# Spreading a column of attention scores over the partitions by two DMAs instead of eight transposes

## The reference, cut to what matters

```python
Wh = einsum('bnf,fo->bno', h, W);  s1 = Wh @ a1;  s2 = Wh @ a2
e = s1[:, :, None] + s2[:, None, :]
e = where(e >= 0, e, 0.2 * e)
e = where(adj == 0, -inf, e);  attention = softmax(e, axis=-1)
h_prime = einsum('bij,bjo->bio', attention, Wh)
```

## Time and profile before

| | us |
|---|---|
| median of 3 runs (638.06 to 638.8) | 638.43 |
| span of the profiled execution, first to last instruction | 636.4 |
| PE busy | 621.6 (98%) |
| DVE busy | 474.8 (75%) |
| ACT busy | 433.8 (68%) |
| POOL busy | 167.4 (26%) |

### The profile page before, as it was taken

The page is one execution under the profiler, slowest core; times in us unless marked ns, Lnnn a source line. Parts: engine busy times, 40 slices in busy tenths (PEclk is TensorE's granted clock), DMA queues, the critical chain, the costliest instruction groups (busy, mean ns, idle before and its releaser), DMA issues.

```text
span 636.4 us, 9580 instructions
## 1 busy us (share of the span) xinstructions
PE 621.6 (98%) x2768; PEld 440.9 (69%) x2768; DVE 474.8 (75%) x1623; ACT 433.8 (68%) x995; POOL 167.4 (26%) x228
## 2 busy tenths in 40 slices
PE   9999999999999999999999999999999999999994
PEld 6756656447975687578658757865885687577794
DVE  4999999876847767866887787688768767465656
ACT  3667767966947766795677577557847766546774
POOL 1464551005233002304503240341143032103211
PEclk9999999999999999999999999999999999999998
DMA  8424000000000000000000000000000000000000
GB/s 337 142 115 166 1 1 1 1 0 2 2 1 1 0 2 0 2 2 33 2 0 2 34 1 2 33 2 1 1 33 2 2 28 6 1 1 33 2 35 33
DMA packets 4372, 16.84 MB, mean 26 GB/s; under 512 B 480, under 2 KB 480, under 8 KB 4192
## 3 DMA queue, kind: packets, MB, share of 16 engines
q1 hardware_dynamic: 4320, 16.23, 6.6%
HBM read 12.03 MB, written 4.19 MB: 26 GB/s over the span
## 4 chain that ended last, share of the span: by engine, by line
PE 76%; DVE 3%; ACT 2%; issue 1%; POOL 0%; POOLq 0%; ACTq 0%; DVEq 0%
PE QQ L831 26%; PE QQ L843 15%; PE PA L814 4%; PE PA L786 4%; PE PB L805 2%; PE PB L796 2%; PE PB L667 2%; PE PA L667 2%; PE PA L767 2%; PE PB L767 2%; PE QQ L865 1%; PE PB L884 1%; PE PB L746 1%; PE PA L746 1%; PE QQ L875 1%
## 5 line engine op out<-in xcount | busy, mean ns | idle before, releaser
L1200 ACT ACTIVATE raw<-QQ,BL 128x256 f32<-128x256 f32 (+2 forms) x279 | 150.1, 558 | 75.1 <-PE QQ L843 37.7
L831 PE MATMUL QQ<-HT,WT 128*128 128x256 f32 (+2 forms) x558 | 183.9, 474 | 1.1 <-ACT raw L1200 0.6
L446 POOL TENSOR_TENSOR RSD<-VAR,pw 128x4 f32<-128x4 f32 (+1 forms) x43 | 61.8, 1438 | 381.7 <-DVE VAR L1422 381.7
L831 PEld LDWEIGHTS QQ<-HT,WT 128*128 128x128 f32 x558 | 103.5, 190 | 59.2 <-issue 28.3
L843 PE MATMUL QQ<-HB,WT 128*128 128x256 f32 (+2 forms) x336 | 100.2, 441 | 0.4 <-DVE HB L1708 0.2
L843 PEld LDWEIGHTS QQ<-HB,WT 128*128 128x128 f32 x336 | 61.2, 190 | 29.3 <-issue 13.4
L1236 ACT ACTIVATE raw<-raw 128x256 f32<-128x256 f32 (+4 forms) x79 | 37.1, 470 | 25.9 <-DVE raw L1690 19.7
L1680 DVE SCALAR_TENSOR_TENSOR raw<-raw 128x256 f32<-128x256 f32 (+2 forms) x60 | 32.5, 542 | 20.2 <-ACT raw L1200 19.6
L1708 DVE SCALAR_TENSOR_TENSOR HB<-raw 128x256 f32<-128x256 f32 (+4 forms) x42 | 20.1, 478 | 23.5 <-ACT raw L1236 23.5
L1042 ACT ACTIVATE X<-Z,OFF,RSD 128x128 f32<-128x128 f32 x80 | 31.8, 482 | 2.0 <-POOL OFF L452 2.0
L512 POOL TENSOR_SCALAR X<-four,MEAN,RSD 128x128 f32<-128x128 f32 x64 | 30.7, 494 | 1.6
(11 more groups left out here) (249 smaller groups left out, 1177.5 us busy)
## 6 DMA issues: line engine op xcount, KB each, us to landing
four<-in_x SPq DMA_DIRECT2D x8, 512.0 KB, 4.0
raw<-in_xt SPq DMA_DIRECT2D x8, 512.0 KB, 6.5
out<-four SPq DMA_DIRECT2D x7, 512.0 KB, 2.6
WT<-in_lstm SPq DMA_DIRECT2D x1, 2048.0 KB, 8.0
later<-in_later SPq DMA_DIRECT2D x1, 725.5 KB, 10.3
AD<-in_adj SPq DMA_DIRECT2D x2, 256.0 KB, 4.8
out<-four SPq DMA_DIRECT2D x2, 256.0 KB, 2.0
early<-in_early SPq DMA_DIRECT2D x1, 275.0 KB, 4.5
```

Source lines behind the costliest of these rows:

```text
L446: pool.tensor_tensor(RSD[kk][:, ts], VAR[kk][:, ts], pw[:, ts], ALU.pow).then_inc(ln[k]["rstd"], some)
L831: mm = pe.matmul(steps_view(Q[q], k), WT[:, 0, (p - 1) * 4 + q, :], ht_view(par, k), start=True, stop=(s == 0))
L1200: act.activation(TG[q][:, at:n], Q[q][:, at:n], ACT.Tanh, scale=0.5 if q == G else 0.25, bias=BL[:, p - 1, q:q + 1]).then_inc(g_ok, 1)
```

## The change

The second score no longer goes through PE. After `a_s12`, SP writes the second half of `S12` to a small tensor in device memory, element by element so that 8 columns become one row of 1,024 numbers, waits until that has landed, and reads the row back into all 128 partitions of an SBUF buffer `ROWS` (a quarter of the input buffer `four` that is free by then). `a_max` waits for this second DMA and reads `ROWS` in place of `PA`. In SP's list both DMAs of a group stand ahead of the sending of the group three before it.

`a_spread1` no longer waits for `a_max` (its buffer `PA` is not used for the rows any more). On DVE `a_max` moves from behind step 3 to behind step 4, and `a_biased0` to between the two halves of step 4. On ACT the first `a_lin` moves from ahead of the gates of step 5 to behind its state.

```diff
+            def spread_scores(g):
+                sp.wait_ge(s12_ok, g - 1)
+                with nc.allow_non_contiguous_dma(reason="a column of scores becomes a row"):
+                    sp.dma_start(scores[g].rearrange("(t p) -> p t", p=P), S12[:, 1, :]).then_inc(column_out, 16)
+                sp.wait_ge(column_out, 16 * (g - 1))
+                sp.wait_ge(ln[2]["out"], TILES * 2)
+                reach(sp, max_ok, TILES * g) if g > 2 else None
+                sp.dma_start(ROWS, scores[g].unsqueeze(0).broadcast_to([P, TILES * P])).then_inc(rows_in, 16)
+
+            spread_scores(2)
             for g in range(GROUPS - 1):
+                spread_scores(g + 3) if g + 3 < GROUPS else None
                 sp.wait_ge(ln[3]["out"], TILES * (g + 1))
...
-            def a_rows(g):
-                pe.wait_ge(s12_ok, g - 1)
-                reach(pe, sp_ok, 2 * g)
-                for b in range(GB):
-                    for c in range(NC):
-                        t = 2 * b + c
-                        mm = pe.transpose(turned(PA, c, b), S12[:, 1, t:t + 1].broadcast_to([P, P]), ident[:])
-                mm.then_inc(s2_ps, 2)
...
-                pe.wait_ge(max_ok, upto(g + 2) * TILES) if g else None
+                reach(pe, sp_ok, 2 * (g + 1)) if g else None
...
-                a_rows(s) if A else None
...
-                a_lin(s, (0,)) if A else None
                 gates(5)
                 a_relu(s - 1) if B else None
                 state(5)
                 if A:
-                    a_lin(s, (1,))
+                    a_lin(s, (0, 1))
                     a_exps(s, (0,))
...
-                dve.wait_ge(s2_ps, halves(g, h))
+                dve.wait_ge(s2_ps, halves(g, h)) if g < 2 else dve.wait_ge(rows_in, 16 * (g - 1))
...
-                rows = f.PB if g < 2 else PA
+                rows = f.PB if g < 2 else ROWS
...
                 cell(3)
-                a_max(s) if A else None
-                cell(4)
+                inner(4)
                 a_biased0(s - 1) if B else None
-                a_bias(s) if A else None
+                state(4)
+                if A:
+                    a_max(s)
+                    a_bias(s)
                 cell(5)
```

More of the change, by code:

```diff
@@ L131, in build @@
         OUT = four[:, 2:4]
+        ROWS = four[:, 1]
         one_a = sb("one_a", [COLS])
@@ L375, in build @@
         half_ps = sem("half_ps")
+        column_out, rows_in = sem("column_out"), sem("rows_in")
+        scores = nc.dram_tensor("scores", (GROUPS, TILES * P), F32, kind="Internal").ap()
         lanes = [Lane(g_ps, g_ok, ca_ok, cf_ok, cell_ok, tc_ok, h_ok, Q, NGATE * LAST + GATE_AT[LANED, I],
@@ L1575, in a_s12 @@
                 dve.wait_ge(ln[1]["rstd"], 2 * (g + 1))
+                reach(dve, column_out, 16 * (g - 2))
                 dve.tensor_tensor(S12[:], DOT[:], RSD[0][:].unsqueeze(1).broadcast_to([P, 2, TILES]), ALU.mult).then_inc(s12_ok, 1)
             def a_max(g, h=None):
-                dve.wait_ge(s2_ps, halves(g, h))
+                dve.wait_ge(s2_ps, halves(g, h)) if g < 2 else dve.wait_ge(rows_in, 16 * (g - 1))
                 reach(dve, att_ps, GB * before(g))
                 f = front(g)
-                rows = f.PB if g < 2 else PA
+                rows = f.PB if g < 2 else ROWS
                 for b in batches(h):
```

## The result

The changed kernel takes 681.79 us, median of 4 runs (681.24 to 683.32), beside 638.26 us for the kernel before on the same chip: a ratio of 1.068, 95% interval 1.067 to 1.070. The forecast was 642.9 us and the range ended at 650. The direction was right and so was the form of one rival, the rows come late; the forecast itself was wrong.

What follows compares the result with a forecast made beforehand. PE, 98% busy, only just covers the chain PE, ACT, DVE, PE, which sets the time at two loads. Transposes 0, new wait 6 x 0.75 = 4.5 us: 636.4 + 4.5 + 2.0 = 642.9 us; range 638.6 to 650.

Steps and rivals of the forecast that it cites:

- the rows come late: Rival: DVE stands at `a_max` waiting for the DMA pair; a slot 0.75 + d longer, 646 us and more; chance 0.23.
- I take 3.5 us: Landing time of the first DMA, 4 KB as 1,024 single numbers; bounds 2.0 to 11.6 us.
- the count of 1,024: The first DMA's number of single numbers, named as speaking for late rows, against the small amount of data.
- The second DMA, taken at 3.2 us: Reading the row back, 512 KB into 128 partitions; bounds 2.6 and 4.1 us.
- the rows that were to be 0.9 us ahead: Rows in SBUF at 328.3, ahead of `a_max` at 329.21; the pair had 7.7 us to land.
- upper bound of 8.1 us late: Most lateness of the rows per slot, if the pair lands at 337.3; the least was 0.
- 6 x 0.75 = 4.5 us: New PE wait at `x(7)` for step 6's state, 0.75 us in each of six slots, from instructions moved on DVE and ACT.
- the transposes' 0 us: Taking 0.87 us of transposes off PE wins nothing, as `x(4)` waits for step 3's state; at most 0.2 us.
- `h(5)` waits 0.48 us as before: On DVE in step 4, `h(5)` gets its state when it got it before; won: nothing.
- the maxima from SBUF at PSUM's price: The eight instructions of `a_max` on DVE keep their 2.75 us when reading SBUF in place of PSUM.
- 1.33 us at `x(4)`: Sign of being right: PE's load for `x(4)` waits about 1.3 us for step 3's state instead of 0.45.
- rival that PE is the bound: The transposes' 0.87 us come off in six slots and `x(7)` does not wait: 633.2 us; chance 0.07.

Runs made afterwards that it cites:

- experiments 5 to 7: Changed kernel, rows from the input, first DMA writing 1,024 numbers 512 bytes apart, only 256 side by side, or 1,024 64 bytes apart: 641.26, 675.58, 641.52 us.
- experiment 3: The kernel before without its eight transposes, nothing in their place and no DMA: 638.96 us, ratio 1.0008.
- 11: Changed kernel with scores turned on DVE, `a_biased0` earlier, two exponentials later, and PE's gap ahead of `x(4)` filled by reordering: 633.12 us beside 638.42, ratio 0.9914.
- 12: The kernel of 11, but the second score spread by eight transposes on PE and maxima read from PSUM: 639.44 us beside 638.64, ratio 1.0013.

## Why the prediction was wrong

**The step that failed** is the first DMA, "I take 3.5 us", out of bounds of 2.0 to 11.6. It took 8.4 to 10.4 us. The value had been set near the low end because of the few bytes; how close the single numbers lie made the time. That the time lies inside the bounds is luck: the upper one adds 60 x 0.16 us for an engine's packets, while all 1,040 packets are handled within about 2 us and the time comes behind them. The rival of late rows came true, though hardly by the count of 1,024 that spoke for it (experiments 5 to 7).

The second DMA, taken at 3.2 us, took 5.1 us in the first three slots and 3.4 to 3.9 in the others. Why it was slower in three of them stays open. The pair was 13.5 to 14.2 us, so the rows that were to be 0.9 us ahead were 5.8 late. By the rival's own form, 638.43 + 6 x (0.75 + 5.8) = 677.7: the path behind the late rows was right. The prediction's own upper bound of 8.1 us late is 691.5 by that form, and its range ended at 650.

**The clock** was in no term. A wait of about 5 us at PE cost its own length and then the slow matmuls behind it, by estimate 5.6 to 5.9 us in all. With 3.0 us for the 4.5 of 6 x 0.75, and 5.6 for the clock, the sum is 681.8; it has to close, since the 5.6 is what was left over, and only the 5.9 is worked out apart from it.

**Right:** the transposes' 0 us (experiment 3); `h(5)` waits 0.48 us as before; the maxima from SBUF at PSUM's price, 421 ns a piece and 419 before; 1.33 us at `x(4)`. **The forecast's own term** of 6 x 0.75 = 4.5 us had the right mechanism and was too large: 3.0 us without the late rows, since ACT caught up 0.45 us at the gates. The prediction's rival that PE is the bound failed for this kernel; with the gap at `x(4)` filled, taking the transposes off PE is worth their whole time (11 and 12).

## What to carry to other kernels

Price a DMA of single numbers by where its pieces land, not by its bytes: written side by side, 4 KB of single numbers landed later (9.2 us) than 512 KB (4.5 us), and a turn on DVE with pieces of 128 bytes took the wait away. Work taken off the busiest engine is worth nothing while the place it leaves is only followed by a wait; look for the wait behind it, fill that, and count again. A duration that contains a wait shrinks when its start is moved later.

## What the hardware showed that was not expected

- 1,024 writes of 4 bytes land in 8.4 to 10.4 us side by side and in 2.5 to 2.7 us 64 bytes apart, with the same count of packets, all handled about 2 us after the issue; 128 writes of 32 bytes land in 1.4 us.
- A maximum on DVE over 256 numbers that lie 32 bytes apart in SBUF takes 615 ns, over neighbours 421.
- After 5.46 us without a load PE ran `h(6)` at half its rate (4.57 us for 2.29, granted clock 0.55), while `a_spread1` behind it already loaded in 3.50 us, as in the earlier trace rows.
